# Turning the key exponentials of layer 0 with VectorE blocks and a scratch in DRAM, and moving one value tile of layer 1 into its batch's first step

## What is computed

```python
# layer 0, h = 8
xn = ln(x) * ln_w + ln_b
q = softmax((xn @ Wq + bq).reshape(b, t, h, 64), axis=-1)
k = softmax((xn @ Wk + bk + (1 - mask) * -1e6).reshape(b, t, h, 64), axis=1)   # over the tokens
v = ((xn @ Wv + bv) * mask).reshape(b, t, h, 64)
att = einsum('bnhd,bnhl->bhdl', k, v)
y = einsum('bnhd,bhdl->bnhl', q, att)
x = x + silu(ln(y) * (1 + scale) + shift) @ W_out + b_out     # scale, shift from cond
# layer 1, h = 16, the same but
att = softmax(einsum('bnhl,bmhl->bnmh', q, k) + (1 - mask) * -1e6, axis=2)
y = einsum('bnmh,bmhl->bnhl', att, v)
```

## Time and profile before

| what | value |
|---|---|
| median of 3 runs | 1324.58 us |
| lowest, highest | 1324.13, 1326.19 us |
| time of the profiled execution | 1324.74 us |
| its span, first to last instruction | 1322.9 us |
| PE busy | 1265.4 us (96%) |
| DVE busy | 1012.7 us (77%) |
| ACT busy | 902.6 us (68%) |
| POOL busy | 499.3 us (38%) |
| layer 0, batches 1 to 6 | 63.7 to 386.7 us |
| layer 1, its 32 steps | from 516.5 us |

### The profile page before, as it was taken

How to read it: one execution, slowest core, us unless ns; L and a number is a source line. 1 busy time by engine, 2 the same in 40 slices (tenths; PEclk the granted TensorE clock), 3 DMA queues, 4 the chain that set the end, 5 groups by cost and what they waited for, 6 DMA issues and landing times.

```text
span 1322.9 us, 24811 instructions
## 1 busy us (share of the span) xinstructions
PE 1265.4 (96%) x9256; PEld 1010.9 (76%) x9256; DVE 1012.7 (77%) x2027; ACT 902.6 (68%) x2051; POOL 499.3 (38%) x451
## 2 busy tenths in 40 slices
PE   8998999999999799899999999999999999999998
PEld 6786888888888687577787788788788788788666
DVE  6678898898988856766876876876876876877766
ACT  5232433424326438788898898898898898898984
POOL 0526548366383730102612612612612512522502
PEclk9998999999999899899999999999999899999989
DMA  9245374664646455855455465464465464454422
GB/s 334 76 152 156 101 222 121 206 194 120 214 127 215 144 197 174 241 164 162 149 172 158 152 174 156 152 175 149 158 174 150 150 182 144 153 172 144 136 75 81
DMA packets 123081, 214.13 MB, mean 162 GB/s; under 512 B 8704, under 2 KB 38456, under 8 KB 122064
## 3 DMA queue, kind: packets, MB, share of 16 engines
q1 hardware_dynamic: 122960, 212.55, 52.1%
HBM read 130.14 MB, written 81.85 MB: 160 GB/s over the span
## 4 chain that ended last, share of the span: by engine, by line
PE 64%; DVE 13%; ACT 11%; POOL 7%; issue 4%; DMA 1%; SPq 0%; DVEq 0%; POOLq 0%; ACTq 0%
PE ps L612 13%; PE ps L613 12%; PE ps L614 12%; PE ps L794 8%; PE ps L768 6%; PE ps L776 6%; ACT ps L958 5%; PE ps L607 3%; DVE st L1080 2%; ACT Pb L968 2%; PE ps L719 2%; POOL yb L1388 2%; DVE xr L1098 2%; POOL yb L1444 1%; POOL vt L1395 1%
## 5 line engine op out<-in xcount | busy, mean ns | idle before, releaser
L958 ACT ACTIVATE ps<-ps,cT 128x512 f32<-128x512 f32 x512 | 346.8, 717 | 19.6 <-DVE cT L1243 19.2
L1243 DVE TENSOR_REDUCE cT<-ps 128x1 f32<-128x512 f32 x512 | 320.6, 682 | 43.8 <-PE ps L768 42.2
L968 ACT ACTIVATE Pb<-ps 128x512 f32<-128x512 f32 x512 | 268.5, 661 | 46.0 <-PE ps L776 43.8
L768 PE MATMUL ps<-Ks,Qs 98*128 98x512 f32 x512 | 185.0, 423 | 16.7 <-ACT ps L958 16.5
L776 PE MATMUL ps<-Qs,Ks 100*128 100x512 f32 x512 | 159.1, 408 | 1.1 <-ACT ps L958 0.5
L768 PEld LDWEIGHTS ps<-Ks,Qs 98*128 98x128 f32 x512 | 96.6, 192 | 67.2 <-ACT ps L958 41.8
L958 ACT ACTIVATION_READ_ACCUMULATOR ps<-ps,cT 128x1 f32 x512 | 134.8, 263 | 0.0
L776 PEld LDWEIGHTS ps<-Qs,Ks 100*128 100x128 f32 x512 | 95.8, 189 | 37.8 <-ACT Pb L968 12.8
L612 PE MATMUL ps<-xTh,Wh_k 128*128 128x512 f32 x256 | 105.6, 413 | 14.0 <-DVE xTl L1102 11.0
L612 PE MATMUL ps<-Wh_o,sTh 128*128 128x512 f32 x256 | 104.7, 409 | 5.1 <-DVE sTl L1220 4.5
L1379 POOL TENSOR_SCALAR vf<-vf,mk 128x512 f32<-128x512 f32 x16 | 25.0, 1564 | 209.7 <-DVE vf L1153 209.7
(11 more groups left out here) (178 smaller groups left out, 2826.3 us busy)
## 6 DMA issues: line engine op xcount, KB each, us to landing
Qs<-stack_scratch SPq DMA_DIRECT2D x32, 768.0 KB
Ks<-stack_scratch SPq DMA_DIRECT2D x32, 768.0 KB
stack_scratch<-sg_q SPq DMA_DIRECT2D x32, 512.0 KB, 2.7
stack_scratch<-sg_k SPq DMA_DIRECT2D x32, 512.0 KB, 2.6
wr<-in_x SPq DMA_DIRECT2D x32, 256.0 KB, 5.0
x_scratch<-wr SPq DMA_DIRECT2D x32, 256.0 KB, 2.4
stack_scratch<-sg_q SPq DMA_DIRECT2D x32, 256.0 KB, 2.9
stack_scratch<-sg_k SPq DMA_DIRECT2D x32, 256.0 KB, 3.0
```

What stands on the lines that cost most here:

```text
L768: e.matmul(bank[:], Qs[par][0:RX, j, t * 128:(t + 1) * 128], Ks[par][0:RX, j, :], start=True, stop=True).then_inc(s["S"], 1)
L958: e.activation(bank[:], bank[:], ACT.Exp, bias=nx[:, n % 2, j, t, 0:1], accum_out=dn[:, b % 2, t, 4 * g + j:4 * g + j + 1]).then_inc(s["S_ ...
L968: e.activation(Pb[m][:, j, :], ps[bank_of["a", n, m, j]][:], ACT.Exp).then_inc(s["P"], 1)
L1243: e.tensor_reduce(nx[:, n % 2, j, t, 0:1], ps[bank_of["S", n, j, t]][:], AX.X, ALU.max, negate=True).then_inc(s["S_max"], 1)
```

## The change

Layer 0: for batches 1 to 6 `ET` is no longer turned by PE. POOL multiplies the exponentials by the reciprocal sums in place (`en`, for all eight batches, a tensor_scalar with one operation), DVE transposes 32 x 32 blocks in place (`ex`, four instructions), and SP takes the result through a new scratch `e_scratch` (`eio`, four stores of 256 KB, one load of 1 MB into `Et`). `sta` then only copies. The channels of the key weights are permuted on the host so that the blocks come to lie right. Batches 0 and 7 still use `te`. DVE's subtraction for `xTl` of quarter c is issued after the scaling of quarter c+1 instead of before it. Layer 1: a value tile may have step g + 4, that is the first step of its own batch, and one of the four does. Some semaphores are merged. The table of positions is new throughout.

```diff
-    "v": ((2, 0.877, 1.032), (3, 0.444, 0.774), (3, 0.763, 0.98), (3, 1.072, 1.08)),
+    "v": ((2, 0.722, 1.004), (2, 0.946, 1.134), (3, 0.791, 0.999), (4, 0.397, 0.661)),
...
-        L0.append((tiles("te", b), *lag(1)))
+        L0.append((tiles("en", b), *lag(14)))
+        if e_by_scratch(b):
+            L0.append((tiles("ex", b), *lag(15)))
+            L0.append(([("eio", b)], *lag(16)))
+        else:
+            L0.append((tiles("te", b), *lag(1)))
...
         for t in X:
-            if more and PLAN["v"][t][0] == g:
-                tracks.append(([("v", 8 + b + 1, t)], *PLAN["v"][t][1:]))
+            step, *pos = PLAN["v"][t]
+            if more and step == g:
+                tracks.append(([("v", 8 + b + 1, t)], *pos))
+            if b and step == g + NG:
+                tracks.append(([("v", 8 + b, t)], *pos))
...
+def e_by_scratch(b):
+
+    return 0 < b < 7
...
             def state(i, b, g):
                 if g == 0:
-                    e.wait_ge(s["E_t"], 4 * b + 4)
+                    e.wait_ge(*((s["e_in"], 16 * b) if e_by_scratch(b) else (s["E_t"], e_turned(b, 3))))
...
-                if i == 1 and turned_on_host(x):
-                    e.wait_ge(s["xT_hi"], 4 * x + c + 1)
-                    e.tensor_tensor(xTl[:, c, :], xr[:, c, :], xTh[:, c, :].bitcast(F32), ALU.subtract).then_inc(s["xT_lo"], 1)
+                if turned_on_host(x):
+                    for u in ((c - 1,) if i == 0 and c else (3,) if i == 1 and c == 3 else ()):
+                        e.wait_ge(s["xT_hi"], 4 * x + u + 1)
+                        e.tensor_tensor(xTl[:, u, :], xr[:, u, :], xTh[:, u, :].bitcast(F32), ALU.subtract).then_inc(s["xT_lo"], 1)
...
+            def en(i, b, t):
+                if t == 0:
+                    e.wait_ge(s["k_exp"], 4 * b + 4)
+                    e.reciprocal(krc[:, b % 2, :], ksm[:, b % 2, :]).then_inc(s["k_rc"], 1)
+
+            def ex(i, b, g):
+                e.wait_ge(s["e_n"], 4 * b + g + 1)
+                e.transpose(E_tile(b, g), E_tile(b, g)).then_inc(s["e_bt"], 1)
+                if g == 3:
+                    mask(b + 1)
...
-                    e.tensor_tensor(A0[r, :, r], part, krc[r, b % 2, :].unsqueeze(2).to_broadcast([64, NC, 64]),
-                                    ALU.mult).then_inc(s["A_c"], 1)
+                    e.tensor_copy(A0[r, :, r], part).then_inc(s["A_c"], 1)
...
+            def en(i, b, g):
+                e.wait_ge(s["k_rc"], b + 1)
+                e.tensor_scalar(E_tile(b, g), E_tile(b, g), krc[:, b % 2, g:g + 1], None, ALU.mult).then_inc(s["e_n"], 1)
...
+            def eio(i, b):
+                if i == 0:
+                    e.wait_ge(s["e_bt"], 4 * b)
+                    if b > 1:
+                        e.wait_ge(s["e_in"], 16 * (b - 1))
+                    blocked = ET[:].rearrange("p g n -> p (g n)").rearrange("p (c n) -> p c n", n=128)
+                    for a in range(4):
+                        e.dma_start(eTd.rearrange("(c r) d -> r c d", r=32)[:, :, 128 * a:128 * a + 128],
+                                    blocked[32 * a:32 * a + 32]).then_inc(s["e_out"], 16)
+                else:
+                    e.wait_ge(s["e_out"], 64 * b)
+                    e.wait_ge(s["att"], b)
+                    e.dma_start(Et[:], eTd.rearrange("(t p) d -> p t d", p=128)).then_inc(s["e_in"], 16)
```

More of the change, by code:

```diff
@@ L85 @@
+    "zstack": ((1.027, 1.118), (0.907, 1.088), (0, 0.34), (0.294, 0.417)),
+    "tle": (None, None, None, (0.477, 0.833)),
+    "zz": ((0.621, 0.811), (0.641, 1.007), (0.865, 1.036), (1.094, 1.15)),
+    "lr": ((0.398, 0.72), None, None, None),
+    "1v": ((0.017, 0.563), (0.376, 1.2), (0.954, 0.987)),
 }
-LAG = (0, 1, 2, 2.5, 3, 3.5, 4, 5, 5.5, 6, 7, 2, 3, 8)
+LAG = (0, 1, 2, 2.5, 3, 3.5, 4, 5, 5.5, 6, 7, 2, 3, 8, 1, 1, 1)
 def weave(order, *tracks):
@@ L477, in e_mod, with E_tile, e_turned @@
             return 16 * L + 4 * (h + 1)
+        def E_tile(b, g):
+            if e_by_scratch(b):
+                return ET[:].rearrange("p g n -> p (g n)").rearrange("p (c g i) -> p c g i", g=NC, i=32)[:, :, g, :]
+            return ET[:, g, :].rearrange("p (c i) -> p c i", i=32)
+        def e_turned(b, t):
+            return b // 7 * 4 + t + 1
         def blocks(buf, x):
@@ L524, in done @@
             if k == "te":
-                return s["E_t"], 4 * key[1] + key[2] + 1
+                return s["E_t"], e_turned(key[1], key[2])
             if k == "ty":
@@ L1145, in v @@
                         e.wait_ge(s["l_bv"], 32)
-                    if x < 8 and t == 0:
-                        e.wait_ge(s["k_exp"], 4 * x + 4)
-                        e.reciprocal(krc[:, x % 2, :], ksm[:, x % 2, :]).then_inc(s["k_rc"], 1)
                     e.wait_ge(s["v_mm"], n)
@@ L1676, in _ @@
             prologue()
[L1677 removed]
+            parts = {"w": w, "m": m, "nx": nx_, "tx": tx, "k": k, "eio": eio, "qio": qio, "yio": yio, "ty": ty, "o": o, "ahead": ahead, "stacks": stacks, "narrow": narrow, "qk": qk,
                      "stack": stack, "nxt": nxt, "lx": lx, "lr": lr, "end": end}
@@ L1698 @@
     P0, P1 = "L0_cond_", "L1_cond_"
+    turn_k = np.arange(D).reshape(4, NC, 32).transpose(1, 0, 2).reshape(D)
     a = {
```

105 lines of the change are left out of this document (49 added, 56 removed), and 14 rows, old and new, of the table PLAN.

## The result

The changed kernel is slower. Its median is 1338.18 us (1335.82 to 1339.71), that of the kernel before, measured beside it, 1324.36 us; the ratio is 1.0104 with a 95% interval of 1.0087 to 1.012. The forecast was 1313 us. The profiled execution took 1335.82 us with a span of 1334.0, 11.1 us more than the 1322.9 before.

What follows compares the result with a forecast made beforehand. PE was taken as the bound, with DVE close behind in layer 0 and ACT setting layer 1's first step. Layer 0 +5, layer 1 -16 and passage -1 gave -12 from 1324.74 us: 1313 us (1304 to 1321; eight in ten 1298 to 1328).

Steps and rivals of the forecast that it cites:

- the first rival: Layer 0 gains too, POOL's multiplications being faster or their delay taken up: batches of 52.5 us, -7, 1301 us; chance 0.28.
- Layer 0, +0.9 a batch: Layer 0: POOL's later row makes the batch about 0.9 us longer instead of 1.8 shorter; +5 us over batches 2 to 6.
- Taken from DVE: the waits of 1.47 and 0.69 us: Layer 0: DVE no longer waits for ACT's high part, as another scaling stands between; 2.2 us off DVE's own loop.
- the waits of PE: Layer 0: PE would wait 3 to 4 us at each batch's first key tile, on xTl.
- The five batches of the forecast: Layer 0: batches 2 to 6 together +5 us, batch 1 given 0 because it already waits on the same chain.
- The trip: Layer 0: the keys' scratch trip, 14 us from the last transpose; PE's 2 us wait at state only moves the later wait.
- Layer 1: Moving the value tile to a step where PE has time gains 2.7 us, seven times, 19 us; -16 with the tail.
- the tail's +3: Layer 1's end: the last batch draws q and k products ahead, so ACT stands idle some 3 us longer.
- the 4 us that PE had to spare: Layer 1, a batch's first step: ACT's 20.3 us against PE's 16.3 leave PE some 4 us for the value tile.
- Passage: Between the layers: the order is mixed anew, a q product fills a wait for the state; -1 us, bounds -5 and +5.
- The third: Slower rival: the keys' trip sets layer 0's batch, +4 us in six batches, +24, 1332 us; chance 0.11.
- Wrong would be DVE waiting for POOL nowhere in layer 0: Layer 0: the sign named to show the prediction wrong, beside layer 1's steps staying at 100 us.

Runs made afterwards that it cites:

- few_turns: l1_only with PE doing 4 instead of 16 turns of the exponentials in each layer 0 batch (output not the reference's): 1314.1 us, ratio 0.9932.
- fill: The changed kernel with 28 useless 512-column matmuls on PE at the first key tile in batches 2 to 7: 1337.3 us, ratio 1.0098.
- old_order: combo with POOL's one-operation ET multiplications and the reciprocal put back where the change has them: 1333.1 us, ratio 1.0073.
- combo: l1_only plus the keys' trip through the scratch, in the old kernel's layer 0 order, ET multiplied with two operations behind the early reciprocal: 1312.9 us, ratio 0.9918.
- tx_early: The changed kernel with one table entry put back, the scalings and subtractions of the next input starting at 0, not 0.135: 1332.6 us, ratio 1.0064.
- all_three: tx_early with the reciprocal also at its old early place and POOL's ET multiplication written with two operations: 1321.4 us, ratio 0.9978.
- after: The changed kernel itself, with the whole change, against the kernel before: 1338.2 us, ratio 1.0104.
- xtl_old: The changed kernel with the xTl subtraction of each quarter back behind its own scaling: 1335.3 us, ratio 1.0085.
- v_moved_alone: The kernel before with only layer 1's fourth value tile moved to the first step of its own batch, other positions old: 1340.6 us, ratio 1.0109.
- l1_only: The kernel before with the changed positions and the moved value tile in layer 1 alone: 1310.3 us, ratio 0.9893.

## Why the prediction was wrong

**What bounds the kernel.** I took PE for the bound of layer 0 because 52.6 us of matmuls filled 53.5, and wrote that DVE is close behind. few_turns shows that taking PE work away gives nothing. Rows 4 and 5 held the loop: POOL's row of 23.8 us and DVE's 26.5 us ahead of it and 3.7 behind it add up to the batch. This misreading lent weight to the first rival, but it did not make the wrong number: the sum of layer 0 did follow the loop's chain to the last `xTl`, and two of its terms were too small.

**Layer 0, +0.9 a batch: the step that failed.** Measured +5.9. Taken from the last `xTl`, the predicted chain was: reciprocal at 22.9, POOL's row from 29.2, 23.0 long, tail 2.4, together 54.6. Measured were 24.6, 31.1, 22.5 and 6.3.
- The tail is the term that was mis-sized most, 3.9 us. I priced what follows the last `xr` instruction (one scaling, ACT, one subtraction) and not what stands in DVE's queue ahead of it. The diff of the table had the cause, one pair going from 0 to 0.135, and the order of DVE showed both first scalings behind `yb`'s transposes and `o`'s addition. I used only the exchange of subtraction and scaling, and counted it as a gain. Even the unchanged tail of the earlier trace rows, from 279.37 to 282.81, is 3.4 us, so 2.4 was 1.0 too short before any change.
- "Taken from DVE: the waits of 1.47 and 0.69 us": they went, and nothing was gained, as the instructions grew by as much.
- The start came 1.9 us later than predicted. 1.3 of it goes with the clock (fill: 29.8), which I had not priced although I forecast the waits of PE that it falls behind (3 to 4 us a batch, measured 4.9).
- Right were the price of a multiplication (1.56 us forecast, 1563 ns measured), the block transposes at 0.71, and the place of the multiplications behind the second value addition:

```profile
L1432 POOL TENSOR_SCALAR ET<-ET,krc 128x512 f32<-128x512 f32 x32 | 49.5, 1563 | 24.7 <-DVE krc L1168 24.7
```

- The five batches of the forecast did not fare alike: batch 2 became 3.3 us longer and 3 to 6 together 23.5, while batch 1, which I gave 0, became 1.2 shorter and what lies ahead of it 1.9 longer.
- By these experiments the 5.9 us of a batch are about 3 for the multiplications' form and place (old_order less combo 3.3, tx_early less all_three 2.6), 1.7 for the place of the scalings (after less tx_early), 0.9 for the order of the subtractions (after less xtl_old; combo's tail against all_three's 1.0), and between -0.2 and +0.6 for the trip. The clock's 1.2 us is no further item; it lies within these. Each is a difference of two single traces and may be off by half a microsecond or more.

**The trip.** Forecast to be hidden, and it is. `Et` landed at 283.5, and PE reached `state` at the same time; the trip from the last transpose took 12.2 us, forecast 14. The first rival's claim that the trip could set a batch of 52.5 (its terms add up to 52.3) was not tested in batches 3 to 6, where the loop came first.

**Layer 1.** Forecast -19 and +3 for the tail, measured -18.3 from its first exponential, of which steps 4 to 28 give 16.0, 2.67 a batch for a forecast 2.7. Of the tail's +3 nothing is seen (101.7 us from step 28 on, 102.3 before). But the reason was half right. I argued from the 4 us that PE had to spare in the old first step, and v_moved_alone shows that this step could not take the tile. The new table made the room: first step 20.3 us, not 27.2. In the old one ACT stood for 4.31 us for the first products and 2.5 for a q product; in the new one it stands for 0.9 in all. PE's waits in that step went from 1.9 to 0.5 us, where I had put them at 4 and 1.5.

**Passage.** -1 forecast, +1.8 measured, within the bounds. In l1_only, with layer 0 as before, it took 128.3 us, so layer 0's new order is not needed for a longer one.

**The rivals.** The third had the sign and nearly the time (1332) with a mechanism that did not happen, so its nearness is luck: it wanted PE to wait over 4 us for `Et` in each batch, and PE does so in batch 1 alone. The true cause was in none of them. "Wrong would be DVE waiting for POOL nowhere in layer 0" did not catch it either: DVE waits for POOL 1.53 us ahead of the tail. What would have caught it is a forecast for when the first quarter of `xr` is scaled.
